# Two cross-attention layers on one core: a PSUM bank moved from the score ring to the maxima ring, one MLP held for the tail, row transfers sent only when needed

## The chip, the cores and the metric

The kernel runs on one core of a Trainium2 chip. The metric is device time in microseconds (us) of one execution; lower is better. Time before: 2152.79 us, the median of three runs (2144.44 to 2155.28). Engines are named as in the profile: PE is TensorE (matmul), PEld its weight load, DVE VectorE, ACT ScalarE, POOL GpSimd, SP the queue that issues most DMAs; a q behind a name is an engine's queue of issues.

## The reference

Two layers on x of 2048 tokens by 256, with a context of 1601 tokens by 256; 16 heads of width 16; an MLP of width 1024.

```python
def layer0(x, c):                       # c: two context tokens
    mod = silu(c) @ ada_w + ada_b       # nine shifts, scales and gates
    x0, x1 = x[:1024], x[1024:]
    x0 += g_msa * mha(mod_(ln(x0)))     # self-attention inside each half
    x1 += g_msa * mha(mod_(ln(x1)))
    ox = attend(q(x0), k(x1), v(x1))    # cross-attention between the halves
    oy = attend(q(x1), k(x0), v(x0))
    x += g_mca * concat(ox, oy) @ proj
    return x + g_mlp * mlp(mod_(ln(x))) # gelu

def layer1(x, ctx, mask):
    x = layernorm(x + self_attention(x, x, mask))
    x = layernorm(x + cross_attention(x, ctx))
    return layernorm(x + relu(x @ w1 + b1) @ w2 + b2)
```

Every attention is a softmax over all its keys. The mask leaves only keys that all queries share; a fast arm of the program, which the given inputs take, uses 512 keys in the masked self-attention.

## The kernel before

**Work and chunks.** Tokens are cut into four chunks of 512 queries. A unit is one chunk and one group of four heads (hg 0 to 3), so each attention has 16 units. A unit runs over key tiles of 128 keys: 8 in each of the two attentions of layer 0, 4 in layer 1's self-attention, 13 in its cross-attention: 256 + 64 + 208 = 528 key tiles in all.

**One key tile.** Scores are made transposed (keys on partitions). Heads are handled in two pairs (`pp` 0 and 1), and one call of `s_step` makes the scores of one pair: two heads in the two row halves of the array (rows 0 to 63 and 64 to 127), each in two accumulating matmuls (line 1488), into two PSUM banks. ACT takes the exponential of each bank (line 1703). After the second pair the product of the tile before with V is made (line 1535, bank 7). Below the two steps of a tile are called A and B, and the heads of them A0, A1, B0, B1 in the order in which their banks are used.

**Maxima.** The softmax subtracts each query's true maximum, which enters the scores as extra rows of Q. So the scores of the next unit are made once more beforehand with the queries on partitions (line 1509), and DVE reduces each 128x512 block (line 1786). `max_tasks` makes these tasks, two blocks each, and `attention` spreads them over the steps of the unit before: the first half of a task stands before the four score matmuls of the step, the second behind them. `fin_a` and `fin_b` then gather the maxima, and ACT's queue issues the transfer that puts them into Q (`QS<-mr`).

**PSUM.** Eight banks of 128x512. Bank 7 is for the product with V. Banks 0 to 3 are the score ring, taken in turn (`a_use`), banks 4 to 6 are a ring for all else (`take_m`): maxima, projections, transposes. A score matmul waits until the exponential that read its bank last is done:

```python
it.bank = [(n["a_use"] + k) % 4 for k in range(2)]
it.a_need = [max(0, n["a_use"] + k - 3) for k in range(2)]
```

`a_need` is a count of exponentials that must be done; the wait stands before the first of a head's two matmuls (`s_half`), and TensorE's queue runs in order.

**The order of the rest.** All queues are written out from one plan in program order. `attention` walks the steps; after every step `bg_step` may take one item from each of two tracks of background work (`work`, `ends_track`): norms, transposes, projections for Q, K and V, output projections, MLPs. Each item of a chain has a number of steps that it waits after the one before (`ln_mod`, `mlp_chain`, `ln_l1`), each chain a unit by which it is due; `bg_until` forces what is due. `later` and `slow` hold DMAs to be issued some steps later: the way of Q and K through DRAM (`split_out` writes, `split_in` reads back as rows, `QS<-scr` and `KS<-scr`) and loads of weights. They are counted down in `fin_step`, and emptied (`flush_later`, `flush_slow`) whenever the next unit to be started is the first of a chunk. `taken` tells that a slot of Q has its rows.

**The tail.** The last chunk of layer 1 is chunk 1. `norm` reciprocates the sums, writes them to DRAM and reads them back spread (`OD<-scr_r`), and `last_l1` does its output projection, norms and MLP with nothing beside them. The MLP of chunk 0 (`mlp1`) runs before that as background work, in both halves.

Of the kernel before, what the change touches and what calls it, by code (L numbers as in the profile page):

```python
# [58 lines left out]
def xattn_kernel(nc, I, out):  # L59
    ctx = ExitStack()  # L60
    with ctx:
# [46 lines left out]
        x = sb("x", [P, NT, D], F32)  # L108
# [67 lines left out]
        n = Counter()  # L176
# [12 lines left out]

        def take_m(it):  # L190

            it.mb = 4 + n["m_use"] % 3
            n["m_use"] += 1
            it.m_need = mark.get(("m_bank", it.mb), [])
            it.m_ready = up("m_ready")
# [31 lines left out]
        def stats_steps(c, eps, b, wait):  # L227
            return [(wait, lambda: do_bn(c, b, 0, 2)), (1, lambda: do_stats(c, eps, b, 0, 4, 2))]

        def xnorm_steps(c, wait):  # L230
            return [(wait, lambda: do_xnorm(c, 0, 2)), (1, lambda: do_xnorm(c, 2, 2))]
# [28 lines left out]
        def do_qk(q, cols, woff, bcol, lo, slot, name, over, buf, quick):  # L260

            def half(oc):
                flush_ends()
                it = item("qk")
                it.q, it.cols, it.woff, it.bcol, it.buf, it.quick, it.oc = q, cols, woff, bcol, buf, quick, oc
                xt_state(it)
                it.w = n["wq_in"] if q else n["wkv_in"]
                it.qf_free = mark.get(("qf_free", quick)) if quick else mark["xn_free"]  # L270
                take_m(it)
                mark["xt_free", buf] = it.m_ready
                mark["wq_free" if q else "wkv_free"] = it.m_ready
                done = "qf_dve" if oc else "qf_act"
                give_m(it, (done, up(done)))

            def split():
                flush_later()
                it = item("split")
                it.q, it.cols, it.quick = q, cols, quick  # L280
                it.f_act, it.f_dve = n["qf_act"], n["qf_dve"]
                it.scr_sem = "scr_q" if quick == 2 else "scr_out"
                it.s3_free = n[it.scr_sem]
                it.hi, it.rest, it.mid, it.low = up("hi_done"), up("rest_done"), up("mid_done"), up("lo_done")
                mark[("qf_free", quick) if quick else "xn_free"] = ("lo_done", it.low)
                ends.append(lambda: split_end(it))
                if quick:
                    flush_ends()
                    quick_rows.append((lambda: to_dram(it), lambda part: to_rows(it, (part,))))
                else:  # L290
                    later.extend([[SPLIT[0], flush_ends], [SPLIT[1], lambda: to_dram(it)]])

            def split_end(of):
                it = item("split_end")
                it.q, it.cols, it.quick = q, cols, quick
                it.rest, it.mid, it.low = of.rest, of.mid, of.low

            def to_dram(of):
                it = item("split_out")
                it.cols, it.low, it.quick = cols, of.low, quick  # L300
                of.k = it.k = 4 + slot if q else n["scr_use"] % 4
                n["scr_use"] += not q
                it.scr_free = mark.get(("scr_free", it.k))
                dma(it, of.scr_sem, 1)
                of.out = it.landed
                if quick:
                    return
                if not q or not taken[slot]:
                    later.append([SPLIT[2], lambda: to_rows(of)])
                else:  # L310
                    assert slot not in held_rows
                    held_rows[slot] = lambda: to_rows(of)

            def to_rows(of, parts=(0, 1)):
                it = item("split_in")
                it.q, it.cols, it.lo, it.slot, it.k, it.out = q, cols, lo, slot, of.k, of.out
                it.scr_sem, it.parts = of.scr_sem, parts
                it.over = [mark[k] for k in [("qs_free", slot)] if k in mark] if q else over
                it.lo_was, it.lo_sem = n[name.replace("in", "lo")], name.replace("in", "lo")
                if 1 in parts:  # L320
                    mark["scr_free", it.k] = (it.lo_sem, up(it.lo_sem, 32))
                    if not q:
                        mark["klo", name] = mark["scr_free", it.k]
                if 0 in parts:
                    dma(it, name, 4)
                    if q:
                        taken[slot] = True
                    else:
                        mark["k", name] = (name, it.landed)

            def second():
                half(1)
                split()
            return [(1, lambda: half(0)), (1, second)]

        def q_steps(c, slot, bc, buf=0, quick=False):
            return do_qk(True, 512, 0, bc, 0, slot, f"q_in{slot}", None, buf, quick)
# [104 lines left out]
        def exp_steps(u, held):  # L442
# [5 lines left out]
            def s_step(i, pp):  # L448
                it = item("s")
                it.u, it.i, it.pp = u, i, pp  # L450
                it.q_in, it.m_in, it.mask = n[f"q_in{u.qs}"], mark["m", u.hg, u.qs], n["mk_step"]
                it.q_lo = n[f"q_lo{u.qs}"]
                it.bank = [(n["a_use"] + k) % 4 for k in range(2)]
                it.a_need = [max(0, n["a_use"] + k - 3) for k in range(2)]
                n["a_use"] += 2
                up("s_ready", 2)
                it.s = [n["s_ready"] - 1, n["s_ready"]]
                if pp == 0:
                    u.slot[i] = n["key_tiles"] % 2
                    n["key_tiles"] += 1  # L460
                it.pt = u.slot[i]
                it.pt_free = mark.get(("pt_free", it.pt), [])
                up("exp_done", 2)
                xs[i, pp] = n["exp_done"]
                if i == len(kts) - 1 and pp == 1:
                    mark["qs_free", u.qs] = ("s_ready", n["s_ready"])
# [247 lines left out]
        taken, held_rows = [False, False], {}  # L714
        quick_rows = []
        slow = []

        def flush_slow():
            while slow:
                slow.pop(0)[1]()  # L720
# [17 lines left out]
        def flush_later():  # L738
            while later:
                later.pop(0)[1]()  # L740
# [52 lines left out]
        def attention(seq, first=True, beyond=(), beside=(), early=None, begun=(), held=None):  # L793
# [25 lines left out]
            for i, (ph, c, qs, hg) in enumerate(seq):  # L819
                u = Unit(ph, c, qs, hg)  # L820
                fg = exp_steps(u, held)
                for f, after in fg[:-1]:
                    if not left and k + 1 < total and (k == 0 or step >= opens[k]):
                        k += 1
                        if every[k][3] == 0:
                            bg_until(unit0[0] + k)
                            flush_later()
                            flush_slow()
                            assert taken[every[k][2]]
                        left = start(k)  # L830
                        m = len(left)
                        lo = step
                        span = max(1, opens[k] - lo)
# [40 lines left out]
            held()  # L874

        def ln_mod(c, g):
            return (stats_steps(c, 1e-6, 0, 4) + xnorm_steps(c, 7 if g == 0 else 3)
                    + [(3, lambda: do_xt("mod", c, g))])

        def kv_l0(c, g, slot=None):  # L880
            over = mark.get("ks_over", []) + mark.get(("half_over", c // 2), [])
            return (ln_mod(c, g) + (q_steps(c, slot, 4 * g) if slot is not None else [])
                    + k_steps(512 * c, 512, f"k_in{c}", over, 4 * g) + v_steps(4 * c, 512, c, over))

        def q_l0(c, slot, g):
# [61 lines left out]
            return ([(4, lambda: do_xt("x", c))] + mlp_chain(c, True, 24, None, (0, 0)) + ln_l1(c, 2, 0)  # L947
                    + [(0, lambda: store(c))])

        def last_l1(c):  # L950

            at["tail"] = True
            flush_norms()
# [7 lines left out]
            do_lnscale(c, 1, 1, 2, 2)  # L961
            for hp in range(1, 4):
                do_hid(c, True, 24, 0, hp)
            do_xt("x", c, cols=256, t0=2)
            do_mout(c, 0, 2, None, (0, 0))
            do_hid(c, True, 24, 1, 0)
# [117 lines left out]
        work.post(8, kv_l0(2, 0))  # L1084
        work.post(8, kv_l0(3, 0))
        work.post(8, q_l0(2, 0, 0), 2)
        work.post(8, q_l0(3, 1, 0) + [(0, lambda: l0_weights("crs"))], 3)
        side.extend([lambda kind=kind, g=g: modulation(kind, g) for g in (1, 2) for kind in ("mod_t", "mod_g")])
        side.append(lambda: gate_bias(0, I["L0_xattn_attn_proj_b"]))
        side.extend([lambda t=t, k=k: scan(t, k) for t in range(NT) for k in range(4)])  # L1090
# [14 lines left out]
        def fast():  # L1105
# [72 lines left out]
            def post_ca(c, qs):  # L1178
                if c == 1:
                    norm(c % 2, True)  # L1180
                    work.post(99, [(0, lambda: need_o("ca")), (None, lambda: last_l1(c))], 2)
                    return
                end_l1(99, c, "ca")
                work.post(99, [(f"ca{c}", lambda: None)] + mlp1(c))

            p1, p3 = phase_l0(1, post), phase_ca(512, 4, post_ca)
# [993 lines left out]
```

## Time and profile before

| | |
|---|---|
| median of three runs | 2152.79 us (2144.44 to 2155.28) |
| the profiled execution's own time | 2160.66 us |
| its span, first to last instruction | 2158.8 us |
| mean granted TensorE clock | 0.957 |
| instructions | 33694 |
| busy, share of the span | PE 91%, DVE 72%, ACT 60%, PEld 36%, POOL 25% |
| moved by DMA | 125.61 MB, 58 GB/s on average |

Durations below come from the one profiled execution, which is 7.9 us above the median. Matmuls overlap in the pipeline and their ends are modelled, so two starts say more than a duration. A share of busy time is a mean over stages with different limits. Of a wait the profile names the releaser that came last.

### The profile page before, as it was taken

To read this page: it belongs to the slowest core of one execution; us is meant where nothing else is said; L and a number is where in the kernel's file an instruction comes from. 1 tells how busy PE (TensorE), PEld (TensorE's weight loads), DVE (VectorE), ACT (ScalarE), POOL (GpSimd) and SP (SyncE) were. 2 spreads that over 40 slices of the span, in tenths; PEclk is the share of its full clock that TensorE was granted. 3 is DMA by queue.
4 is the path that set the end of the run, shared out by engine and by line. 5 is a ranking of instruction groups with operands and counts; after the bars stand their busy time and mean duration, and the time that the engine had idled before them with its cause. 6 is when DMAs were issued, how large, how long until landed. Compare 5 with 4: busy or idle time off the path is not lost. (4 is left out here: it accounts for less than half of the span.)

```text
span 2158.8 us, 33694 instructions
## 1 busy us (share of the span) xinstructions
PE 1969.9 (91%) x12890; PEld 767.6 (36%) x12890; DVE 1559.6 (72%) x2905; ACT 1293.2 (60%) x2406; POOL 540.9 (25%) x409
## 2 busy tenths in 40 slices
PE   5899799898989999999988998899999999999976
PEld 3333233232323343433524433222335235335325
DVE  4767788787967858568365567888994995996804
ACT  1146576565756676757766655457874874784660
POOL 1135784572032311022111334302010101101100
PEclk9689999999999999999999999889999999999998
DMA  6724423432044302033043444220020020000000
GB/s 152 146 82 112 127 69 85 106 80 50 17 117 73 80 21 56 16 66 72 3 106 60 98 108 100 63 46 19 7 48 3 17 44 3 14 17 4 14 17 12
DMA packets 96249, 125.61 MB, mean 58 GB/s; under 512 B 25261, under 2 KB 80926, under 8 KB 90958
## 3 DMA queue, kind: packets, MB, share of 16 engines
q1 hardware_dynamic: 93774, 122.84, 24.2%
q8 instruction: 103, 1.69, 0.3%
q10 hardware_dynamic: 2304, 0.53, 0.1%
q14 instruction: 68, 0.56, 0.1%
HBM read 88.90 MB, written 24.74 MB: 53 GB/s over the span
## 5 line engine op out<-in xcount | busy, mean ns | idle before, releaser
L1703 ACT ACTIVATE PT<-ps 128x512 f32<-128x512 f32 (+1 forms) x2112 | 1109.6, 601 | 649.8 <-PE ps L1488 631.6
L1786 DVE TENSOR_REDUCE mx<-ps 128x1 f32<-128x512 f32 x2048 | 1281.9, 681 | 206.4 <-PE ps L1509 203.6
L1488 PE MATMUL ps<-QS,KS 51*128 51x512 bf16 (+3 forms) x4224 | 809.0, 385 | 15.9 <-DMA QS<-mr 15.5
L1509 PE MATMUL ps<-KS,QS 49*128 49x512 bf16 x2048 | 730.6, 392 | 94.5 <-DVE mx L1786 52.7
L1535 PE MATMUL ps<-PT,Vt 128*32 128x512 f32 (+1 forms) x4224 | 575.4, 617 | 0.0
L1509 PEld LDWEIGHTS ps<-KS,QS 49*128 49x128 bf16 x2048 | 188.4, 94 | 679.1 <-DVE mx L1786 433.6
L1488 PEld LDWEIGHTS ps<-QS,KS 51*128 51x128 bf16 (+3 forms) x4224 | 236.7, 96 | 235.5 <-ACT PT L1703 57.8
L2057 POOL TENSOR_TENSOR OD<-ON,OD 128x1024 f32<-128x1024 f32 x15 | 35.4, 2359 | 488.8 <-DMA OD<-scr_r 488.8
L1535 PEld LDWEIGHTS ps<-PT,Vt 128*32 128x32 f32 (+1 forms) x4224 | 83.8, 108 | 143.6 <-issue 141.3
L1630 PE MATMUL ps<-XT,big 128*128 128x256 f32 x512 | 123.9, 392 | 4.2 <-ACT big L1759 3.6
L1642 PE MATMUL ps<-big 128*128 128x256 f32 x512 | 114.6, 382 | 1.6 <-DVE big L1930 1.6
L1594 PE MATMUL ps<-XT,wA 128*128 128x512 f32 (+1 forms) x216 | 108.0, 626 | 6.7 <-ACT xn L1741 4.3
L2041 POOL CAST S<-xn 128x1024 bf16<-128x1024 f32 (+1 forms) x26 | 26.2, 1009 | 345.3 <-issue 223.5
L1630 PEld LDWEIGHTS ps<-XT,big 128*128 128x128 f32 x512 | 95.1, 192 | 42.3 <-ACT big L1759 20.2
L1642 PEld LDWEIGHTS ps<-big 128*128 128x128 f32 x512 | 96.0, 190 | 21.8 <-DVE mx L1786 5.5
L2096 POOL TENSOR_SCALAR big<-big 128x512 bf16<-128x512 int32 x64 | 96.7, 1513 | 13.5 <-DMA big<-in_mask_1x1xSxS_ik 13.5
L2066 POOL TENSOR_TENSOR x<-x,xn 128x512 f32<-128x512 f32 x24 | 30.5, 1271 | 263.5 <-DVE xn L1897 263.4
L1618 PE MATMUL ps<-wP,OD 128*128 128x256 f32 x256 | 68.5, 427 | 21.8 <-DVE OD L1886 11.3
L2029 POOL TENSOR_SCALAR rs<-mv 128x4 f32<-128x4 f32 (+2 forms) x32 | 7.3, 229 | 293.5 <-DVE mv L1817 293.3
L1897 DVE TENSOR_TENSOR xn<-ps,G 128x512 f32<-128x512 f32 x24 | 16.6, 692 | 85.0 <-PE ps L1642 52.2
L2099 POOL TENSOR_TENSOR big<-big 128x512 bf16<-128x512 bf16 x60 | 69.3, 1155 | 5.0
L1901 DVE TENSOR_TENSOR x<-ps,x 128x512 f32<-128x512 f32 (+1 forms) x25 | 16.8, 670 | 73.1 <-PE ps L1642 50.4
(110 smaller groups left out, 1112.6 us busy)
## 6 DMA issues: line engine op xcount, KB each, us to landing
scr<-S SPq DMA_DIRECT2D x27, 768.0 KB, 3.8
big<-in_mask_1x1xSxS_ik SPq DMA_DIRECT2D x16, 1024.0 KB, 5.8
QS<-scr SPq DMA_DIRECT2D x32, 384.0 KB, 9.3
KS<-scr SPq DMA_DIRECT2D x24, 384.0 KB, 8.7
QS<-scr SPq DMA_DIRECT2D x32, 256.0 KB, 6.1
ON<-Oe SPq DMA_DIRECT2D x256, 32.0 KB, 2.0
OD<-scr_r SPq DMA_DIRECT2D x32, 256.0 KB
KS<-scr SPq DMA_DIRECT2D x24, 256.0 KB, 4.9
```

The source lines that it names most:

```text
L1488: z = eng.matmul(ps[0:w, it.bank[1 - j], :], KS[lo:hi, part, pr, col:col + w], QS[lo:hi, part, u.qs, pr, :], start=part == 0, stop=part == ...
L1509: return eng.matmul(mbank(it)[:, 0:w], QS[lo:lo + MR, 0, u.qs, pr, 128 * it.tq:128 * it.tq + 128], KS[lo:lo + MR, 0, pr, it.lo:it.hi], sta ...
L1535: z = eng.matmul(ps[32 * j:32 * j + 32, 7, :], Vt[0:w, vt, lo:lo + 32], PT[0:w, it.pt * 4 + j, :], start=it.i == 0, stop=it.i == len(u.kts ...
L1594: z = eng.matmul(mbank(it)[:, 0:it.cols], wA[:, a, lo:lo + 128], XT[it.buf][:, a, 0:it.cols], start=a == 0, stop=a == 1)
L1618: z = eng.matmul(mbank(it)[:, 256 * t:256 * t + 256], OD[:, a, lo:lo + 128], wP[:, a, :], start=a == 0, stop=a == 1)
L1630: z = eng.matmul(mbank(it)[:, 256 * i:256 * i + 256], w1[:, a, lo:lo + 128], XT[0][:, a, 256 * it.hf:256 * it.hf + 256], start=a == 0, sto ...
L1642: z = eng.matmul(mbank(it)[:, 256 * t:256 * t + 256], HT[:, hc, lo:lo + 128], w2[:, hc, :], start=hc == 0, stop=hc == 7)
L1703: eng.activation(PT[0:w, it.pt * 4 + 2 * it.pp + 1 - k, :], ps[0:w, it.bank[k], :], ACT.Exp, scale=0.25).then_inc(S["exp_done"], 1)
L1786: eng.tensor_reduce(out=mx[:, u.b, c, it.i:it.i + 1], in_=mbank(it)[:, 0:it.hi - it.lo], axis=AX.X, op=ALU.max).then_inc(S["max_done"], 1)
L2057: eng.tensor_tensor(od, ON[:, :, it.lo:it.hi], od, ALU.mult).then_inc(S["ot_done"], 1)
L2096: eng.tensor_scalar(dst, src, 0.0, None, ALU.is_equal).then_inc(S["scan_acc"], 1)
L2099: eng.tensor_tensor(ac, ac, dst, ALU.add).then_inc(S["scan_acc"], 1)
```

## The change

- The score ring has three banks (0 to 2) and the ring of maxima and projections four (3 to 6).
- The MLP of chunk 0 in layer 1 is cut: `mlp1_first` does its first half as background work once the last unit has begun (`"last"`), `between` does the second half in the tail while the normalisation's transfers run, and its last norm and store go into `last_l1` behind the hidden groups of the last chunk's first half.
- At the first unit of a chunk `later` and `slow` are emptied only if the slot has no rows yet or keys that it needs are still to be sent (`due_keys`).
- The norm chains of the second round (g = 1) wait a step less at each stage, and each chain of K and V begins by emptying `slow`. The load of the cross-attention weights is put on `slow`, six steps later at the earliest.

```diff
 def take_m(it):
-            it.mb = 4 + n["m_use"] % 3
+            it.mb = 3 + n["m_use"] % 4
@@ do_qk, split / to_rows
+                if not q:
+                    due_keys.add(("k", name))
...
+                        due_keys.discard(("k", name))
@@ s_step
-                it.bank = [(n["a_use"] + k) % 4 for k in range(2)]
-                it.a_need = [max(0, n["a_use"] + k - 3) for k in range(2)]
+                it.bank = [(n["a_use"] + k) % 3 for k in range(2)]
+                it.a_need = [max(0, n["a_use"] + k - 2) for k in range(2)]
@@ attention
+                if i == len(seq) - 1:
+                    ended.add("last")
...
                             bg_until(unit0[0] + k)
-                            flush_later()
-                            flush_slow()
+                            if not taken[every[k][2]] or any(key in due_keys for key in every[k][0].kdep(every[k][1])):
+                                flush_later()
+                                flush_slow()
@@ ln_mod, kv_l0
-            return (stats_steps(c, 1e-6, 0, 4) + xnorm_steps(c, 7 if g == 0 else 3)
-                    + [(3, lambda: do_xt("mod", c, g))])
+            return (stats_steps(c, 1e-6, 0, 4 if g != 1 else 3) + xnorm_steps(c, 7 if g == 0 else 3 if g == 2 else 2)
+                    + [(3 if g != 1 else 2, lambda: do_xt("mod", c, g))])
...
-            return (ln_mod(c, g) + (q_steps(c, slot, 4 * g) if slot is not None else [])
+            return ([(0, flush_slow)] + ln_mod(c, g) + (q_steps(c, slot, 4 * g) if slot is not None else [])
@@ the tail
+        def mlp1_first(c):
+            return [(4, lambda: do_xt("x", c))] + [(hp % 2, lambda hp=hp: do_hid(c, True, 24, 0, hp)) for hp in range(4)] + [
+                (2, lambda: do_mout(c, 0, 2, None, (0, 0)))]
+
+        def between(c):
+            flush_outs()
+            for f in norms[:2]:
+                f[1]()
+            del norms[:2]
+            for hp in range(4):
+                do_hid(c, True, 24, 1, hp)
+            do_mout(c, 2, 2, None, (0, 0))
+
-        def last_l1(c):
+        def last_l1(c, other=()):
...
             for hp in range(1, 4):
                 do_hid(c, True, 24, 0, hp)
+            for f in other:
+                f()
@@ the posts
-        work.post(8, q_l0(3, 1, 0) + [(0, lambda: l0_weights("crs"))], 3)
+        work.post(8, q_l0(3, 1, 0) + [(0, lambda: slow.append([6, lambda: l0_weights("crs")]))], 3)
...
-                    work.post(99, [(0, lambda: need_o("ca")), (None, lambda: last_l1(c))], 2)
+                    work.post(99, [(0, lambda: need_o("ca")), (0, lambda: between(0)),
+                                   (None, lambda: last_l1(c, [f for _, f in ln_l1(0, 2, 0)] + [lambda: store(0)]))], 2)
                     return
                 end_l1(99, c, "ca")
+                if c == 0:
+                    work.post(99, [("ca0", lambda: None), ("last", lambda: None)] + mlp1_first(c))
+                    return
```

## Rows read from the trace of the kernel before

**Rows 1.** The page: busy us, share of the span, instructions.
```profile
PE 1969.9 (91%) x12890; PEld 767.6 (36%) x12890; DVE 1559.6 (72%) x2905; ACT 1293.2 (60%) x2406; POOL 540.9 (25%) x409
```

**Rows 2.** The page's groups by line: count | busy us, mean ns | idle before, releaser.
```profile
L1703 ACT ACTIVATE PT<-ps 128x512 f32<-128x512 f32 (+1 forms) x2112 | 1109.6, 601 | 649.8 <-PE ps L1488 631.6
L1786 DVE TENSOR_REDUCE mx<-ps 128x1 f32<-128x512 f32 x2048 | 1281.9, 681 | 206.4 <-PE ps L1509 203.6
L1488 PE MATMUL ps<-QS,KS 51*128 51x512 bf16 (+3 forms) x4224 | 809.0, 385 | 15.9 <-DMA QS<-mr 15.5
```

**Rows 3.** Timeline of a steady tile: start us, us, engine, what, count [idle before].
```profile
1519.86 11.23 DVE L1786 TENSOR_REDUCE mx<-ps 128x1 f32<-128x512 f32 x18
...
1523.20 0.39 PE L1509 MATMUL ps<-KS,QS 49*128 49x512 bf16 x1
...
1523.87 0.81 PE L1488 MATMUL ps<-QS,KS 51*128 51x512 bf16 x4
...
1524.38 0.39 PE L1509 MATMUL ps<-KS,QS 49*128 49x512 bf16 x1
...
1524.69 1.07 PE L1535 MATMUL ps<-PT,Vt 128*32 128x512 f32 x8
...
1525.69 0.39 PE L1509 MATMUL ps<-KS,QS 49*128 49x512 bf16 x1
```

**Rows 4.** Timeline of PE in the last unit, starts of three tiles.
```profile
2067.79 1.04 PE L1488 MATMUL ps<-QS,KS 51*128 51x512 bf16 x8
...
2069.76 1.45 PE L1488 MATMUL ps<-QS,KS 51*128 51x512 bf16 x8
...
2072.14 1.04 PE L1488 MATMUL ps<-QS,KS 51*128 51x512 bf16 x8
```

**Rows 5.** Timeline of PE, 1524.25 to 1524.30: the tile's sixth and seventh score matmuls.
```profile
1524.09 0.38 PE L1488 MATMUL ps<-QS,KS 51*128 51x512 bf16 x2
```

**Rows 6.** Timeline of ACT, 1524.0 to 1524.3: the exponential of A0.
```profile
1523.91 0.60 ACT L1703 ACTIVATE PT<-ps 128x512 f32<-128x512 f32 x1 [0.42 <-PE ps L1488]
```

**Rows 7.** Timeline of ACT, 2070.07 to 2070.4: one exponential in the last unit.
```profile
2069.94 0.62 ACT L1703 ACTIVATE PT<-ps 128x512 f32<-128x512 f32 x1
```

**Rows 8.** Timeline of weight loads in the same tile of the last unit.
```profile
2070.61 0.11 PEld L1488 LDWEIGHTS ps<-QS,KS 51*128 51x128 bf16 x3 [0.40 <-ACT PT L1703]
2071.14 0.16 PEld L1535 LDWEIGHTS ps<-PT,Vt 128*32 128x32 f32 x8 [0.43 <-issue]
```

**Rows 9.** Groups of PE by line: the projections and MLPs.
```profile
L1630 PE MATMUL ps<-XT,big 128*128 128x256 f32 x512 | 123.9, 392 | 4.2 <-ACT big L1759 3.6 <-DVE XT L1837 0.6
L1642 PE MATMUL ps<-big 128*128 128x256 f32 x512 | 114.6, 382 | 1.6 <-DVE big L1930 1.6
L1594 PE MATMUL ps<-XT,wA 128*128 128x512 f32 (+1 forms) x216 | 108.0, 626 | 6.7 <-ACT xn L1741 4.3 <-issue 0.9 <-ACT XT L1728 0.8
L1618 PE MATMUL ps<-wP,OD 128*128 128x256 f32 x256 | 68.5, 427 | 21.8 <-DVE OD L1886 11.3 <-POOL OD L2057 9.4 <-DVE mx L1786 1.0
L1606 PE MATMUL ps<-wA,XT 128*128 128x256 f32 (+1 forms) x180 | 44.6, 391 | 1.0 <-DVE mx L1786 0.2
```

**Rows 10.** Waits of PE: us in total, times, longest.
```profile
PE ps L1509 <- DVE mx L1786: 52.7, 111, 1.4
PE ps L1488 <- DMA QS<-mr: 15.5, 3, 7.6
...
PE ps L1618 <- DVE OD L1886: 11.3, 1, 11.3
```

**Rows 11.** Timeline of the tail.
```profile
2102.34 6.52 PE L1618 MATMUL ps<-wP,OD 128*128 128x256 f32 x16 [11.29 <-DVE OD L1886]
...
2124.46 7.17 PE L1642 MATMUL ps<-big 128*128 128x256 f32 x32 [0.53 <-DVE big L1930]
...
2131.47 7.07 PE L1630 MATMUL ps<-XT,big 128*128 128x256 f32 x32
```

**Rows 12.** Busy us by stretch: PE, PEld, DVE, ACT, POOL, granted clock, DMA share, GB/s.
```profile
1374.00:1425.00 51.00, 42.14 (x199) 11.60 (x199) 40.78 (x79) 14.78 (x27) 12.29 (x8) 0.77 0.13 30
```

More of the change, by code:

```diff
@@ L716, in xattn_kernel @@
         slow = []
+        due_keys = set()
         def flush_slow():
```

## The prediction

> **What bounds the kernel now.** I read the page's busy times first. TensorE (PE) is busy for 91% of the span [rows 1]; VectorE (DVE) and ScalarE (ACT) have 72% and 60%, but those are means over stages. The groups by line say what the bulk is: 4224 score matmuls of line 1488 and 2048 matmuls for maxima, each of these with one reduction on DVE of 681 ns [rows 2]. A key tile takes eight score matmuls, so there are 4224 / 8 = 528 key tiles. Nearly everything hangs on what one of them costs.
>
> The timeline of one steady tile is the view that decides [rows 3]. The tile begins at 1523.20 with a maxima matmul beside the scores of the first head pair (step A: heads A0, A1), goes on at 1523.87 with the second pair (step B: B0, B1), reaches its last maxima matmul at 1524.38, the product with V at 1524.69, and the next tile begins at 1525.69: 2.49 us. DVE runs 18 reductions in 11.23 us without a break, 0.624 us each; four a tile are 2.50 us. So here DVE sets the pace, and PE waits a little for a bank of the maxima ring.
>
> How little is shown by the last unit, which has no maxima [rows 4]. Two of its tiles begin at 2067.79 and 2069.76: 1.97 us where nothing waits. Four maxima matmuls ride in pairs with others, row half beside row half, which adds two slots of about 0.22 us (the second pair of the steady tile starts at 1523.87, the half after it at 1524.09 [rows 3, 5]). That is 2.41 us, so a steady tile has only 0.08 us of waiting for DVE in it.
>
> **Part 1: three score banks.** A step writes two banks. With four of them a score matmul waits for the exponential of four uses before; with three, of three uses before. Counting uses A0=0, A1=1, B0=2, B1=3: B1 now shares a bank with A0 of the same tile, and may start only when A0's exponential is over. In program order only two maxima matmuls stand between the two steps, if no projection does.
> Where that stands in the trace: A0's exponential starts at 1523.91, 0.71 us after the tile, and takes 0.60 us [rows 6], so it ends at +1.31. B1's first matmul now starts at 1524.09, at +0.89 [rows 5]. From the end of an exponential to the matmul it releases it is 0.05 us: one ends at 2069.94 + 0.62 = 2070.56 [rows 7], and the weights behind it load at 2070.61 [rows 8]. So B1 moves from +0.89 to +1.36. TensorE takes its queue in order: B0's second half, the last maxima matmul and the product with V are queued behind it. From the released matmul to the product with V it is 2071.14 - 2070.61 = 0.53 us [rows 8], and from there to the next tile 1525.69 - 1524.69 = 1.00 us [rows 3]. New tile: 1.36 + 0.53 + 1.00 = 2.89 us instead of 2.49, so 0.40 us more. DVE then has 2.50 us of work in 2.89 and is no longer the limit; a serial loop of PE, ACT and PE takes its place. The other new pairings are free: the next A0 needs A1's exponential, over at about +1.8, and the next A1 needs B0's, over at about +2.45.
>
> In how many tiles? A projection queued between A and B covers the wait. The projections by line are 216/4 + 180/8 + 256/8 + 512/8 + 512/32 = 54 + 22 + 32 + 64 + 16 = 188 items [rows 9]; each is started after a step, so about half fall between A and B, and with transposes I take 100 tiles spared. 428 x 0.40 = 171 us. From it comes off what PE idles today for a maxima bank, 52.7 us [rows 10], because in a longer tile DVE is never that far behind: 118 us. In the 13 tiles of the last unit the loop is as long, 2.89, against a mean of (2072.14 - 2067.79) / 2 = 2.18 us [rows 4], 0.71 instead of 0.40: 4 us more. Part 1 is worth **+122 us**.
> Bounds. Below: what a ring wait costs in this kernel today, a tile of 2.38 beside one of 1.97 [rows 4], 0.21 a tile: 428 x 0.21 - 52.7 = 37 us. Above: no tile spared and nothing taken off, 528 x 0.40 = 211 us. I stay with the chain worked out above, since each link has its own row; the lower end would need A0's exponential to be earlier than it is.
>
> **Part 2: four banks for maxima and projections.** A deeper ring lets PE run one reduction, 0.62 us, further ahead. In the steady tile DVE has no time left, so depth gives nothing; elsewhere it gives at most the 52.7 us already taken off. Beyond that: 0, from -10 (idle behind evictions of projections) to 0.
> The Trainium skill, Perfetto Trace Analysis, section "Matmuls", says that independent matmul groups should rotate through different PSUM banks so that the eviction of one overlaps the next group. It does not say which of two rings should have the eighth bank; the trace has 0.08 us of wait in the one that gains and 0.47 us of new wait in the one that loses. Taken for the maxima ring alone, the rule would make this change a gain.
>
> **Part 3: the MLP held for the end.** Today PE idles 11.3 us in the tail until the normalised output is there [rows 10], then runs 16 records in 6.52 us [rows 11] where the mean group has 68.5 / 256 = 0.27 us a record, 4.3 us [rows 9]. The held half is four hidden matmul groups (32 records) and one output group (32), 7.07 + 7.17 = 14.2 us of PE [rows 11], taken out of the stretch before. In the tail 11.3 us of it are hidden, 3 us stick out, and some 4 us come back because the work that follows runs at full clock (6.52 to 4.3, and the first transposes and hidden groups too). Against it: statistics, scaling and store of chunk 0 now stand in DVE's and SP's queues in the tail, about 7 us of DVE behind the last hidden group, beside the 7.17 us output group. The evictions and both norm transfers are issued on SP before the held matmuls, so nobody waits for them longer. Net **-12 us**, from -19 to 0. The first half of that MLP moves into the last unit, where the ring wait covers some of it; this is inside the bound.
>
> **Part 4: steps earlier, transfers later.** The delays of the second-round norm chains shrink by a step each; steps get 16% longer, so in time they stay. If one comes early, PE waits for the norm at a transpose. Row transfers are no longer flushed at every fourth unit but only if the query slot or the keys are due, and the cross-attention weights wait six steps. All of this is on SP's queue; what it collides with is the transfer of the maxima's rows, issued by ACT, for which PE waits 15.5 us in three places [rows 10]. Two of the three would go at best, with some half-clock time behind them: **-10 us**, from -25 to +10 (a flush comes late and PE waits for the rows instead).
>
> **Sum.** 122 + 0 - 12 - 10 = +100 us. The profiled execution took 2160.7 us (span 2158.8), 7.9 above the median of the three runs, so 2261 by its account and **2253 us** as a median: 4.6% slower. A measurement of this kernel can tell about 0.5%, 11 us.
>
> **Rivals.**
> *The maxima ring pays* (0.10, faster). The steady tile is DVE's, the wait for A0 costs nothing because PE would have waited anyway, and the fourth bank takes away the 52.7 us: 2153 - 53 - 12 - 10 = 2078 us. For it: DVE unbroken over 18 reductions [rows 3]. Against it: it decides at +0.89 us into the tile; A0's exponential would have to be over by then, and it ends at +1.31.
> *The ring wait is mostly covered* (0.07). Waits on DVE upstream and downstream of B1 absorb it down to the lower bound: 2153 + 37 - 22 = 2168 us; with a little more cover it is no change.
> *The clock falls as well* (0.07, slower). Where maxima keep PE waiting for DVE, from 1374 to 1425 us, PE is busy 42.1 of 51 us, 83%, at a granted clock of 0.77 [rows 12]; the new steady tile has 2.41 of 2.89 us, also 83%. If 23% of the attention ran at 1.2 instead of 2.4 GHz, with a tile then about 1.9 us longer (PE's 2.41 us twice, less the 0.48 of ring wait that this covers), 428 x 0.44 = 188 us would be added: 2440 us. Against it: there the matmuls come singly, here twelve halves stand close together with one gap of 0.3 us. The Trainium skill, TensorE: Matmul & The Clock Gate, section "Part 1: The HAM clock gate", has the clock follow how busy the engine has been recently; by it the new tile, with PE at work in most of it, would keep its clock.
> That parts 3 or 4 don't do what they say would move the time by their own bounds only.
>
> **How the numbers follow.** The forecast has 0.76, the rivals 0.10, 0.07 and 0.07. Own range of the forecast: part 1 with cover a third better or worse (80 to 165), parts 3 and 4 at their bounds: about 2185 to 2315. The covered case at 2168 is taken in, which leaves 0.17 outside: 2165 to 2315. Slower by over 0.5%: 0.76 + 0.07 and part of the covered case, 0.85; within 0.5%: 0.05; faster: 0.10.
>
> **What would show it.** In the changed profile: a steady tile of 2.89 us; the pair of step B split, with weights of line 1488 idle about 0.4 us before them, released by ACT; DVE with gaps, its reductions no longer unbroken; waits of PE for DVE near zero; PE's idle or stretched time spread evenly over the attention. In the tail no 11 us gap, hidden and output matmuls in its place. It would be wrong if the steady tile stays at 2.49 us, or if B1 starts before A0's exponential has ended.

## The result, and the profile after

The changed kernel takes 2252.28 us, the median of four runs (2248.51 to 2259.27), against 2152.81 us for the kernel before: ratio 1.0463, 95% interval 1.0441 to 1.0486, 4.6% slower. The forecast was 2253 us. The profiled execution took 2248.65 us, 88 us more than the one before, and lies 3.6 us under its median where the one before lay 7.9 us above.

The page of the changed kernel, busy times and the groups that answer to [rows 1, 2] (lines of the code moved down by 26: 1514 is 1488, 1535 is 1509, 1561 is 1535, 1729 is 1703, 1812 is 1786):

```profile
PE 1971.0 (88%) x12890; PEld 715.8 (32%) x12890; DVE 1561.3 (69%) x2908; ACT 1333.7 (59%) x2406; POOL 533.2 (24%) x406
...
L1729 ACT ACTIVATE PT<-ps 128x512 f32<-128x512 f32 (+1 forms) x2112 | 1145.6, 594 | 682.2 <-PE ps L1514 679.0
L1812 DVE TENSOR_REDUCE mx<-ps 128x1 f32<-128x512 f32 x2048 | 1277.6, 680 | 280.8 <-PE ps L1535 276.8
L1514 PE MATMUL ps<-QS,KS 51*128 51x512 bf16 (+3 forms) x4224 | 875.0, 386 | 158.4 <-ACT PT L1729 149.1
```

No instruction got longer, and PE is busy for as long as before (1971.0 against 1969.9 us). What is new is idle time ahead of the scores: 158.4 us where it was 15.9, and 149.1 of it ended by an exponential. The waits of PE, to be read against [rows 10] (us in total, times, longest):

```profile
PE ps L1514 <- ACT PT L1729: 149.1, 398, 3.7
PE ps L1535 <- DVE mx L1812: 21.5, 54, 3.9
PE ps L1609 <- POOL x L2108: 12.3, 6, 3.3
...
PE ps L1514 <- DMA QS<-mr: 8.3, 2, 5.2
```

The waits for DVE fell from 52.7 to 21.5 us, and 398 waits of the scores for ACT stand where there was none. One steady tile shows all of it. Timeline of the changed kernel (start us, us, engine, what, count, idle before):

```profile
1600.23 0.39 PE L1535 MATMUL ps<-KS,QS 49*128 49x512 bf16 x1
...
1600.66 2.48 DVE L1812 TENSOR_REDUCE mx<-ps 128x1 f32<-128x512 f32 x4 [0.41 <-PE ps L1535]
...
1600.90 0.38 PE L1514 MATMUL ps<-QS,KS 51*128 51x512 bf16 x1
1600.94 2.17 ACT L1729 ACTIVATE PT<-ps 128x512 f32<-128x512 f32 x4 [0.73 <-PE ps L1514]
1601.60 0.60 PE L1514 MATMUL ps<-QS,KS 51*128 51x512 bf16 x3 [0.32 <-ACT PT L1729]
...
1602.13 1.07 PE L1561 MATMUL ps<-PT,Vt 128*32 128x512 f32 x8
1603.13 0.39 PE L1535 MATMUL ps<-KS,QS 49*128 49x512 bf16 x1
```

The tile is 1603.13 - 1600.23 = 2.90 us, against 2.49 in [rows 3]. B0's first matmul still starts in its old place (1600.90); then three matmuls wait until 1601.60, 1.37 us into the tile, released by ACT; the product with V follows 0.53 us later. DVE, whose reductions ran without a break in the kernel before, now has a gap of 0.41 us in every tile. The last unit, which has no maxima, has a tile of 2153.86 - 2150.97 = 2.89 us instead of the 1.97 and 2.38 of [rows 4]:

```profile
2150.97 0.82 PE L1514 MATMUL ps<-QS,KS 51*128 51x512 bf16 x5
2152.32 0.60 PE L1514 MATMUL ps<-QS,KS 51*128 51x512 bf16 x3 [0.53 <-ACT PT L1729]
2152.86 1.06 PE L1561 MATMUL ps<-PT,Vt 128*32 128x512 f32 x8
2153.86 0.82 PE L1514 MATMUL ps<-QS,KS 51*128 51x512 bf16 x5
```

In the tail the 11.29 us gap of [rows 11] is filled, but not as neatly as forecast:

```profile
2172.21 7.17 PE L1656 MATMUL ps<-XT,big 128*128 128x256 f32 x32
2180.44 7.14 PE L1668 MATMUL ps<-big 128*128 128x256 f32 x32 [1.06 <-DVE big L1956]
2189.70 5.41 PE L1644 MATMUL ps<-wP,OD 128*128 128x256 f32 x16 [2.11 <-DVE OD L1912]
```

The last product with V ends at about 2172.2, the output projection starts at 2189.7: 17.5 us, where it was 11.3. The held groups take 15.4 us with a gap of 1.06 us among them, and 2.1 us are lost because DVE multiplies the normalised output (`OD`, line 1912) only after the residual of the held half, which stands ahead of it in its queue.

### The profile page after: what moved, and what is told of

Same layout as the page of the kernel before. It is cut to its first block and busy times, and to the rows that moved or that the text cites. A ratio compares the mean times of both kernels' runs of the same rounds, so it can differ in the third digit from the quotient of the medians.

```text
span 2246.8 us, 33711 instructions
## 1 busy us (share of the span) xinstructions
PE 1971.0 (88%) x12890; PEld 715.8 (32%) x12890; DVE 1561.3 (69%) x2908; ACT 1333.7 (59%) x2406; POOL 533.2 (24%) x406
## 5 line engine op out<-in xcount | busy, mean ns | idle before, releaser
L1729 ACT ACTIVATE PT<-ps 128x512 f32<-128x512 f32 (+1 forms) x2112 | 1145.6, 594 | 682.2 <-PE ps L1514 679.0
L1514 PE MATMUL ps<-QS,KS 51*128 51x512 bf16 (+3 forms) x4224 | 875.0, 386 | 158.4 <-ACT PT L1729 149.1
L1535 PE MATMUL ps<-KS,QS 49*128 49x512 bf16 x2048 | 711.1, 389 | 40.9 <-DVE mx L1812 21.5
L1514 PEld LDWEIGHTS ps<-QS,KS 51*128 51x128 bf16 (+3 forms) x4224 | 213.8, 95 | 491.9 <-ACT PT L1729 393.0
L1668 PE MATMUL ps<-big 128*128 128x256 f32 x512 | 123.0, 402 | 2.7 <-DVE big L1956 2.7
L1668 PEld LDWEIGHTS ps<-big 128*128 128x128 f32 x512 | 102.3, 203 | 24.3 <-issue 5.6
L1785 ACT ACTIVATE big<-ps,colb 128x256 f32<-128x256 f32 x96 | 39.4, 472 | 52.5 <-PE ps L1656 52.2
```

Source lines behind the costliest of these rows:

```text
L1514: z = eng.matmul(ps[0:w, it.bank[1 - j], :], KS[lo:hi, part, pr, col:col + w], QS[lo:hi, part, u.qs, pr, :], start=part == 0, stop=part == ...
L1535: return eng.matmul(mbank(it)[:, 0:w], QS[lo:lo + MR, 0, u.qs, pr, 128 * it.tq:128 * it.tq + 128], KS[lo:lo + MR, 0, pr, it.lo:it.hi], sta ...
L1668: z = eng.matmul(mbank(it)[:, 256 * t:256 * t + 256], HT[:, hc, lo:lo + 128], w2[:, hc, :], start=hc == 0, stop=hc == 7)
L1729: eng.activation(PT[0:w, it.pt * 4 + 2 * it.pp + 1 - k, :], ps[0:w, it.bank[k], :], ACT.Exp, scale=0.25).then_inc(S["exp_done"], 1)
L1785: z = eng.activation(HT[:, hc, :], mbank(it)[:, 256 * i:256 * i + 256], ACT.Relu if it.relu else ACT.Gelu_apprx_tanh, bias=colb[:, it.bc + ...
```

## The experiments

All are the kernel before or after with one part changed. Times are medians; ratios are to runs of the kernel before on the same chip, whose medians were 2153 to 2158 us; brackets hold the 95% interval of a ratio. Some figures below come from counting tiles in the profiled executions: a tile goes from its first score matmul to that of the next, and a plain tile is one in which no projection, MLP matmul or transpose runs. There are 353 of them in each of the kernels so compared.

**1. The rings alone.**

```diff
-            it.mb = 4 + n["m_use"] % 3
+            it.mb = 3 + n["m_use"] % 4
-                it.bank = [(n["a_use"] + k) % 4 for k in range(2)]
-                it.a_need = [max(0, n["a_use"] + k - 3) for k in range(2)]
+                it.bank = [(n["a_use"] + k) % 3 for k in range(2)]
+                it.a_need = [max(0, n["a_use"] + k - 2) for k in range(2)]
```

> Edit: the kernel before with only the two bank rings changed, three banks for scores and four for the rest. My theory (the second pair of scores waits for the exponential of the first): a steady tile of 2.90 us as in the changed kernel, and all of the loss plus what parts 3 and 4 give back, 2265 to 2280 us. Rival theory (the loss comes from the transfers and chains that were moved): 2150 to 2180 us, and a steady tile near 2.49 us.

Measured: 2259.47 us, ratio 1.0489 (1.0452 to 1.0526), +106 us. Its timeline has the changed kernel's tile:

```profile
1602.14 0.39 PE L1509 MATMUL ps<-KS,QS 49*128 49x512 bf16 x1
...
1602.81 0.38 PE L1488 MATMUL ps<-QS,KS 51*128 51x512 bf16 x1
1603.51 0.60 PE L1488 MATMUL ps<-QS,KS 51*128 51x512 bf16 x3 [0.32 <-ACT PT L1703]
```

The released matmuls start 1.37 us into the tile. The whole loss is in the rings; it is 6 us less than my range allowed. The rest of the change gives back 7 us by the medians, not 22, and even 7 is within the noise, for the intervals of 1.0489 and 1.0463 overlap.

**2. All but the rings.** The changed kernel with the two hunks above reversed.

> Edit: the changed kernel with the old rings, four banks for scores and three for the rest; the held MLP, the row transfers by need and the shorter delays stay. My theory: steady tile back at 2.49 us, 2125 to 2140 us, 0.6 to 1.3% under the kernel before. Rival theory (parts 3 and 4 are part of the loss): above 2165 us. In between, 2145 to 2160, they do nothing.

Measured: 2144.56 us, ratio 0.9956 (0.9938 to 0.9975). The steady tile is back at 2.49 us. A gain, so parts 3 and 4 are no part of the loss, but 9 us (0.44%) instead of 22, and outside the range that I gave it.

**3. Three score banks, three for the rest.**

```diff
-                it.bank = [(n["a_use"] + k) % 4 for k in range(2)]
-                it.a_need = [max(0, n["a_use"] + k - 3) for k in range(2)]
+                it.bank = [(n["a_use"] + k) % 3 for k in range(2)]
+                it.a_need = [max(0, n["a_use"] + k - 2) for k in range(2)]
```

> Edit: the kernel before with three banks for scores, and still three for the rest; one PSUM bank lies idle. It tells what the fourth bank of the maxima ring is worth. My theory: in the steady tile DVE has time to spare, so the fourth bank gives 0 to 10 us: 2265 to 2290 us, tile 2.90 us. Rival (the maxima ring of four gives back a good part of what the score ring costs): 2300 us or more.

Measured: 2282.54 us, ratio 1.0600 (1.0562 to 1.0638), +130 us. So the score bank costs 130 us, and the fourth bank of the other ring gives back 2282.5 - 2259.5 = 23 us. That is more than the 0 to 10 us that I gave it, and far from paying for the move. Its waits of maxima matmuls for DVE are 27.8 us beside 18.0 in run 1, and those for a bank that ACT has to empty after an MLP group, 7.4 us, are not among the longer waits of run 1:

```profile
PE ps L1488 <- ACT PT L1703: 129.5, 382, 3.1
PE ps L1509 <- DVE mx L1786: 27.8, 73, 1.3
...
PE ps L1509 <- ACT big L1759: 7.4, 9, 1.2
```

By the count of tiles the whole gain of the fourth bank lies in plain tiles: 1076 us in run 3, 1051 in run 1, with a median of 2.90 us in both. 43 of them are over 0.3 us shorter in run 1, 28 us together. In 37 of these 43, DVE has over 1 us of work other than reductions of scores (norm statistics and scaling above all) between 1.5 us before the tile and its end; of the other 310 this is so in 16. One such tile in run 3:

```profile
1932.36 0.39 PE L1509 MATMUL ps<-KS,QS 49*128 49x512 bf16 x1
...
1932.99 0.73 DVE L1812 BATCH_NORM_STATS2 st<-x 128x6 f32<-128x256 f32 x2
...
1933.75 0.38 DVE L1817 BATCH_NORM_AGGREGATE mv<-st 128x2 f32<-128x6 f32 x4
...
1934.77 0.39 PE L1509 MATMUL ps<-KS,QS 49*128 49x512 bf16 x1 [0.43 <-DVE mx L1786]
...
1936.08 0.39 PE L1509 MATMUL ps<-KS,QS 49*128 49x512 bf16 x1
```

The norm statistics hold back the reductions, the tile's last maxima matmul waits for its bank, and the tile takes 3.72 us. In run 1 the same tile has a fourth bank to go on with, and takes 2.90 us.

**4. Two score banks, five for the rest.**

```diff
-            it.mb = 4 + n["m_use"] % 3
+            it.mb = 2 + n["m_use"] % 5
-                it.bank = [(n["a_use"] + k) % 4 for k in range(2)]
-                it.a_need = [max(0, n["a_use"] + k - 3) for k in range(2)]
+                it.bank = [(n["a_use"] + k) % 2 for k in range(2)]
+                it.a_need = [max(0, n["a_use"] + k - 1) for k in range(2)]
```

> Edit: the kernel before with two banks for scores and five for the rest, so that the suspected wait doubles. My theory, worked from the changed tile: B0 now waits for A0's exponential (1.36 us into the tile) and B1 for A1's, over at 1.80, so it starts at 1.85; the product with V follows 0.53 us later and the next tile 1.00 us after that: 3.38 us a tile, 0.49 more than with three banks; times 428 tiles is 210 us over the run with three banks, about 2480 us. Rival (the loss is not from the score ring): within 20 us of the run with three banks.

Measured: 2422.42 us, ratio 1.1251 (1.1208 to 1.1294), 163 us over three banks. The tile came out as worked:

```profile
1701.63 0.39 PE L1509 MATMUL ps<-KS,QS 49*128 49x512 bf16 x1
...
1702.99 1.09 PE L1488 MATMUL ps<-QS,KS 51*128 51x512 bf16 x4 [0.32 <-ACT PT L1703]
...
1704.02 1.06 PE L1535 MATMUL ps<-PT,Vt 128*32 128x512 f32 x8
1705.02 0.64 PE L1488 MATMUL ps<-QS,KS 51*128 51x512 bf16 x4
```

B0 is released at +1.36 (1702.99), the product with V starts at +2.39, the tile is 3.39 us. The time did not: 163 us, not 210. The 353 plain tiles went from 1051 to 1214 us, 0.46 each; 74 tiles with a projection or transpose only after the start of step B grew by 0.24 us each, and the 100 that have one before it got 0.22 us shorter each. So the price of a steady tile was right and the count of 428 was too high.

**5. The held MLP alone.** The kernel before with `mlp1_first`, `between`, the new `last_l1` and the posts of the change, and nothing else of it.

> Edit: the kernel before with only the MLP of chunk 0 in layer 1 cut and its second half, last norm and store held for the tail (old rings, old transfers, old delays). My theory was -12 us for this part, after the run of all but the banks (-8 us for both parts) rather -5 to -12: 2141 to 2148 us. Rival (the DVE work and the two extra stores in the tail eat it up, and the gain is from the transfers): 2150 us or more.

Measured: 2144.70 us, ratio 0.9946 (0.9926 to 0.9965), 11.7 us less. In its tail the projection runs at full clock:

```profile
2084.06 3.72 PE L1643 MATMUL ps<-wP,OD 128*128 128x256 f32 x16 [2.11 <-DVE OD L1911]
```

It took 6.52 us before [rows 11] and takes 5.41 in the changed kernel, where a stretch at half clock begins at 2189.9. From the start of the projection to the end of the span it is 55.1 us in this run, 56.4 in the kernel before and 57.1 in the changed kernel.

**6. The transfers and delays alone.** The kernel before with `due_keys`, `flush_slow` ahead of each chain of keys, the weights on `slow` and the shorter delays.

> Edit: the kernel before with only the row transfers by need, the cross-attention weights put off, and the delays of the second-round norms a step shorter (old rings, old tail). My theory was -10 us for this part; after the run of all but the banks rather 0 to -5: 2147 to 2153 us, with less waiting of PE for the transfer of the maxima rows than the 15.5 us of before. Rival: it costs what the tail gains, 2155 us or more.

Measured: 2159.17 us, ratio 1.0007 (0.9985 to 1.0028). The part does what it is for and gains nothing: the time lies above my range and in that of the rival, but the kernel before took 2157.96 us on the same chip. Its waits of PE:

```profile
PE ps L1514 <- DVE mx L1791: 55.5, 108, 5.2
...
PE ps L1623 <- POOL OD L2062: 9.9, 2, 9.2
PE ps L1493 <- DMA QS<-mr: 8.9, 3, 6.1
```

The wait for the rows of maxima fell from 15.5 to 8.9 us; the longest wait for DVE rose from 1.4 to 5.2 us. Whether that one wait is what takes the gain back is not shown.

**7 and 8. ReLU for GELU in layer 0's MLP, with and without the new rings.** The changed kernel has waits that no steady tile has. ACT loads a table when it turns from exponential to GELU and back, 24 times each way. (With ReLU in layer 0's MLP the two kernels of this section compute something else than the reference; they only measure what the tables cost, and have one table load instead of 49.) Timeline of the changed kernel:

```profile
765.50 1.28 ACT L1785 ACT_TABLE_LOAD   x1
...
766.79 0.84 ACT L1785 ACTIVATE big<-ps,colb 128x256 f32<-128x256 f32 x2
...
767.65 1.28 ACT L1729 ACT_TABLE_LOAD   x1
768.94 1.09 ACT L1729 ACTIVATE PT<-ps 128x512 f32<-128x512 f32 x2
769.59 0.76 PE L1514 MATMUL ps<-QS,KS 51*128 51x512 bf16 x3 [2.62 <-ACT PT L1729]
```

The exponential of A0 stands behind 1.28 + 0.84 + 1.28 us of GELU and tables, and B1 behind it: PE idles 2.62 us. The changed kernel has eight such waits of 2.6 to 3.7 us, 24 us together.

```diff
-                                               ACT.Relu if it.relu else ACT.Gelu_apprx_tanh,
+                                               ACT.Relu,
```

> Edit: the kernel with only the two rings changed, and layer 0's MLP with ReLU in place of GELU (the function of the reference is changed there; shapes and engines stay). In the kernel with the rings of three and four, PE waits eight or so times 2.6 to 3.7 us for an exponential that stands behind a GELU and two loads of ACT's table of 1.28 us. Theory: with three score banks these switches are exposed, some 20 us; the run falls by 20 us more than the same edit takes off the kernel before, to about 2225 us. Rival: the waits are shorter elsewhere, and the edit takes the same off both.

> Edit: the kernel before with layer 0's MLP with ReLU in place of GELU (the function is changed there). Theory: with four score banks most of the table switches are hidden; 2138 to 2150 us, and a difference to the run with three score banks and ReLU of 80 to 90 us instead of 106. Rival: it falls as much as the other, and the difference stays at 106 us.

Measured: 2218.18 us, ratio 1.0292 (1.0258 to 1.0326), with the new rings; 2145.67 us, ratio 0.9948 (0.9927 to 0.9969), without. The edit takes 2.0% off the first (1.0489 to 1.0292) and 0.5% off the second, so about 1.5%, 31 us, of the 106 us of the rings is exposed table switching; the four intervals leave some 12 us either way. I had expected 20 us, and 80 to 90 us between the two ReLU kernels, where it is 72.5. The count of tiles says the same: in the tiles that are not plain, ReLU takes 40 us off the kernel with the new rings and 11 us off the kernel before, in the plain ones 1 and 4. The waits of PE for an exponential in run 7 are all short:

```profile
PE ps L1488 <- ACT PT L1703: 126.3, 386, 1.3
```

The difference of the two ReLU kernels, 1.0292 - 0.9948 = 3.4% or 74 us, is what the rings cost without table switches.

**9 and 10. GELU groups four at a time.** Runs 5 and 7 point to a version that might beat both kernels.

```diff
-                    + [(hp % 2, lambda hf=hf, hp=hp: do_hid(c, relu, bc, hf, hp)) for hp in range(1, 4)]
+                    + [(hp % 2 if relu else 0, lambda hf=hf, hp=hp: do_hid(c, relu, bc, hf, hp)) for hp in range(1, 4)]
```

> Edit: the kernel with only the held MLP (0.9946 of before), and the four hidden groups of a GELU half started in one step instead of two and two, so that ACT changes its table half as often there. Theory: the switches cost this kernel at most what ReLU takes off it, 12 us, so half of that at best: 2134 to 2145 us against a before of 2153 to 2158. Rival: four groups in a row keep DVE from its maxima for 7 us and three banks run out, the time is 5 to 20 us longer than with the held MLP alone.

> Edit: the changed kernel with the same grouping of GELU halves. Theory: with three score banks the table switches cost some 30 us (the difference between the two ReLU edits), and half of the switches is gone: 10 to 15 us less than the changed kernel, 2236 to 2246 us, with half as many waits of 2.6 us and more of scores for an exponential. Rival: 2250 us or more, because what counts is not the number of switches but the long stay of PE in other work.

Measured: the held MLP with grouped GELU 2140.97 us, ratio 0.9922 (0.9907 to 0.9936), the fastest kernel of the study; beside 0.9946 for the held MLP alone the intervals overlap, so the grouping itself is not shown to help there. The changed kernel with the same edit: 2239.13 us, ratio 1.0382 (1.0367 to 1.0397), 0.8% under 1.0463, and those intervals are apart. That is in the range I gave. The table loads fell from 49 to 17, which is more than half, the long waits from eight of up to 3.7 us to four of 1.9 us:

```profile
PE ps L1514 <- ACT PT L1729: 137.8, 399, 1.9
```

## Why the prediction was right, and where it was not

**Part 1, three score banks.** The mechanism and the size of a tile were right to 0.01 us: B1 forecast at +1.36 and measured at +1.37, product with V 0.53 later, tile 2.89 forecast and 2.90 measured; with two banks 3.38 forecast and 3.39 measured. (The list of pairings leaves one out, the next B0 behind B1's exponential. It is free too: that one is over at 1603.11 in the changed kernel, and the next B0 starts at 1603.80.) The term of 122 us met 130 us in run 3, but its factors were less good than their sum. There are 353 plain tiles, not 428. Of these, 254 had taken at most 2.6 us before, and they grew by 109 us in run 3, 0.43 each; the other 99 had been longer already, and changed by 3 us in all. The 52.7 us of waiting for DVE, taken off whole, fell only to 27.8 in run 3. And a cost is missing in the prediction: some 31 us of table switches on ACT, hidden by four score banks and exposed by three. I had costed the other queue on the new loop, ACT's, by its exponentials alone. That these errors nearly cancel in 122 us is luck; the 0.40 us of a tile are not.

**Part 2, four banks for the rest.** This term was mis-sized: "0, from -10 to 0" beyond the DVE waits already taken off, and 23 us measured as a whole (run 3 less run 1). In the steady tile depth gives nothing, as forecast, for the medians of both runs are 2.90 us. The gain lies in plain tiles whose reductions start late, most often because DVE has norm work to do first (run 3). The reason given in the prediction, that DVE has no time left, is not what runs 1 and 3 test, for DVE idles in their steady tiles; a fourth maxima bank beside four score banks was not run, since with the bank for V that makes nine. Parts 1 and 2 together are +106 us against 122.

**Part 3, the held MLP.** Forecast -12, measured -12 alone (-8 to -16 by the interval). The steps differ: the held work pushes the output projection out by 6 us, not 3, since the multiplication by the reciprocals waits in DVE's queue behind the held residual. The queue that the held work is put ahead of was the one to look at. And of the 4 us that the full clock was to give back, run 5 shows 1.3 from the projection to the end, the changed kernel none. With the forecast's 14.2 us taken out of the stretch before, that leaves -9 us, inside the interval.

**Part 4, transfers and delays.** This step failed: -10 forecast, nothing measured (1.0007). PE was to lose two of its three waits for `QS<-mr`; three are still there in run 6, 8.9 us together instead of 15.5 (in the changed kernel two, 8.3 us), and the time did not follow even by that. Why it did not stays open.

**The sum** was 122 - 12 - 10 = +100 us and is +99.5. That it is so close is luck. Parts 1 and 2 together cost 16 us less than forecast (8 more for the score bank, 23 less for the maxima bank), and parts 3 and 4 gave some 15 us less: all but the rings is worth 9 us on the old rings and 7 on the new (2259.5 to 2252.3), not 22. One thing that was to show it did not come true: the waits of PE for DVE were to be near zero and are 21.5 us.

**The rivals.** That the maxima ring pays (2078 us) is ruled out by run 3: it gives 23 us against 130. The covered case (2168 us) is ruled out by run 1: +106 us from the rings, with the whole 0.41 us in the steady tile. The clock did not fall: its mean is 0.958, it was 0.957, and from 1600 to 1680 us it is at full speed, with PE busy in 71 of 80 us:

```profile
1600.00:1680.00 80.00, 71.26 (x558) 20.65 (x555) 66.53 (x123) 56.11 (x104) 10.86 (x7) 1.00 0.18 35
```

The Trainium skill, Perfetto Trace Analysis, section "Matmuls", has independent matmul groups rotate through different PSUM banks. Each ring by itself bears it out: a bank taken from the scores cost 130 us, and a bank given to the maxima gave 23. Here it was the ring with the longer way back, matmul to exponential to matmul, 1.36 us, that needed the bank more than the one whose reader, DVE, was busy all through the steady tile.

## What to carry to other kernels

Before a buffer is moved from one ring to another, write down for each ring which use shares it after the move and what stands between the two in the queue of the engine that waits; the distance in time from the start of the first to its release, less the work between, is the new cost of each round. Here a single tile of the timeline gave it to a hundredth of a microsecond; how many rounds pay it was the harder question, and only a count of the tiles answers it. Look for the worth of depth not in the steady tile but where the ring's reader has other work first: the fourth maxima bank changed nothing in the median tile, and took 0.8 us off one in which DVE had norm statistics to make. Price the reader's other work too (a change of activation table, an eviction), for a shallower ring shows every delay that a deeper one had hidden.

## What had not been expected of the hardware

A change of ACT between exponential and GELU costs a table load of 1.28 us each way, 48 of them in this kernel, 62 us of ACT. Four score banks let most of it pass (replacing GELU gained 0.5%); with three, replacing GELU gained 2.0%.
